# A language-model tower on one core: moving the row-maximum loop by two slots, reordering three engines' work, and weighing the low-rank product with ScalarE and GpSimd

## The reference, cut to what matters

```python
h = einsum('bsk,kh->bsh', concat[pos[s], nest[nesting(x)], seg[segments(x)]], W)     # 32 x 512 x 128
h = h + attn(layernorm(h))       # 8 heads of 16, softmax over 512 keys, no mask
# experts, on the layernorm of h (xf): 4 experts, rank 16
weights = relu(softmax(xf @ gate_w.T) - sigmoid(xf @ thr_w.T) / 4); weights /= sum(weights)
hidden = relu(einsum('ni,ehi->neh', xf, fc1_w))
lo = einsum('neh,ehr->ner', hidden, lora_A)                  # "low" in the kernel
out = einsum('ne,ned->nd', weights, fc2(lora_B(lo)))         # weights are applied to lo in the kernel
h = h + out
```

## Time and profile before

| | before |
|---|---|
| median of 3 runs | 1198.49 us (1197.38 to 1198.84) |
| the profiled execution, own time / span | 1197.47 / 1195.7 us |
| busy: PE, DVE, ACT, POOL | 88%, 80%, 69%, 57% of the span |
| granted TensorE clock, mean of the span | 0.957 (1.00 from 110 to 1150 us) |

### The profile page before, as it was taken

One profiled execution on the slowest core, in us unless ns is written; L12 is line 12 of the kernel. 1 busy time (PEld: TensorE's weight loads), 2 busy tenths in 40 slices (PEclk: granted clock), 3 DMA queues, 4 the chain that ended last, 5 costly groups with the idle time before them and its releaser, 6 DMA issues.

```text
span 1195.7 us, 20256 instructions
## 1 busy us (share of the span) xinstructions
PE 1052.9 (88%) x6158; PEld 393.8 (33%) x6158; DVE 952.5 (80%) x2442; ACT 821.4 (69%) x1578; POOL 681.9 (57%) x684
## 2 busy tenths in 40 slices
PE   5268889999999999999999999999999999999965
PEld 2012233333333333333333333333333333333322
DVE  7399888888888888888888888888888888888322
ACT  2216777777777777777777777777777777776841
POOL 1844575676556665665566665765556656632231
PEclk8558999999999999999999999999999999999986
DMA  2544545554544445555544455545544455541111
GB/s 73 136 100 107 126 105 129 125 121 118 126 120 112 112 119 135 119 121 121 128 114 112 115 122 133 118 120 123 127 109 113 116 130 122 121 98 39 55 56 36
DMA packets 93242, 132.43 MB, mean 111 GB/s; under 512 B 18109, under 2 KB 69822, under 8 KB 86918
## 3 DMA queue, kind: packets, MB, share of 16 engines
q1 hardware_dynamic: 91584, 129.54, 45.1%
q10 hardware_dynamic: 1550, 1.59, 0.5%
HBM read 89.20 MB, written 35.01 MB: 104 GB/s over the span
## 4 chain that ended last, share of the span: by engine, by line
PE 53%; DVE 25%; issue 9%; ACT 8%; DMA 3%; POOL 1%; SPq 0%; POOLq 0%; ACTq 0%; DVEq 0%
PE pv L723 13%; PE mix L733 13%; DVE negmax L1009 10%; PE sc L710 9%; PE mix L787 7%; ACT probs L578 4%; PE mix L770 3%; PE mix L808 3%; PE mix L792 3%; DVE bn L999 2%; DVE qk L994 2%; ACT hid L632 2%; DVE out_sb L1088 2%; DVE h_sb L986 2%; DVE h L1034 2%
## 5 line engine op out<-in xcount | busy, mean ns | idle before, releaser
L1009 DVE TENSOR_REDUCE negmax<-mix 128x1 f32<-128x512 f32 x1024 | 671.9, 680 | 122.7 <-PE mix L733 119.6
L578 ACT ACTIVATE probs<-sc 128x512 f32<-128x512 f32 x1024 | 574.3, 596 | 218.2 <-PE sc L710 214.1
L733 PE MATMUL mix<-kstk,qstk 96*128 96x512 bf16 x1024 | 360.2, 395 | 84.0 <-ACT turned L622 22.4
L710 PE MATMUL sc<-qstk,kstk 120*128 120x512 bf16 x1024 | 361.7, 381 | 1.5 <-ACT probs L578 1.2
L723 PE MATMUL pv<-probs,vals 128*32 128x512 f32 x2048 | 273.8, 601 | 0.0
L733 PEld LDWEIGHTS mix<-kstk,qstk 96*128 96x128 bf16 x1024 | 92.3, 98 | 434.7 <-DVE negmax L1009 179.1
L514 POOL TENSOR_TENSOR ctxh<-ctx_sb,rdenb 128x512 f32<-128x512 f32 x64 | 81.2, 1270 | 221.0 <-DMA rdenb<-rden_dram 220.6
L787 PE MATMUL mix<-xn2T,fc1T_sb 128*128 128x512 f32 x256 | 135.4, 612 | 8.0 <-DVE negmax L1009 8.0
L710 PEld LDWEIGHTS sc<-qstk,kstk 120*128 120x128 bf16 x1024 | 99.7, 98 | 103.7 <-issue 29.8
L494 POOL TENSOR_TENSOR qk<-qk,rstdb 128x512 f32<-128x512 f32 x64 | 81.3, 1272 | 92.0 <-DMA rstdb<-rstd_dram 92.0
L632 ACT ACTIVATE hid<-mix 128x512 f32<-128x512 f32 x128 | 76.1, 596 | 35.4 <-PE mix L787 35.4
(11 more groups left out here) (141 smaller groups left out, 1067.4 us busy)
## 6 DMA issues: line engine op xcount, KB each, us to landing
stack_dram<-pieces SPq DMA_DIRECT2D x192, 128.0 KB
rdenb<-rden_dram SPq DMA_DIRECT2D x64, 256.0 KB
qstk<-stack_dram SPq DMA_DIRECT2D x32, 384.0 KB, 6.6
kstk<-stack_dram SPq DMA_DIRECT2D x32, 384.0 KB, 8.7
rstdb<-rstd_dram SPq DMA_DIRECT2D x32, 256.0 KB, 3.4
qstk<-stack_dram SPq DMA_DIRECT2D x32, 256.0 KB, 7.0
kstk<-stack_dram SPq DMA_DIRECT2D x32, 256.0 KB, 9.2
wrow<-w_dram SPq DMA_DIRECT2D x32, 256.0 KB
```

Of the source, the lines that this page charges most:

```text
L578: act.activation(probs[:, c % 8, i % 2], sc[:, i % RING], ACT.Exp).then_inc(s_exp, 1)
L710: pe.matmul(sc[:, i % RING, :], kstk[0:KROWS, u, h, j * P:(j + 1) * P], qstk[0:KROWS, u, h, :], start=True, stop=True).then_inc(s_score, 1)
L733: pe.matmul(max_bank(m), qstk[0:STK, u, h, j * P:(j + 1) * P], kstk[0:STK, u, h, :], start=True, stop=True).then_inc(s_mxmm, 1)
L1009: dve.tensor_reduce(negmax[:, m // NT, m % NT:m % NT + 1], max_bank(m), AX.X, ALU.max, negate=True).then_inc(s_max, 1)
```

## The change

It has five parts. (1) `MSTART` goes from 8 to 10. (2) PE: `fc1_3` goes to slot 1 and `embed` to slot 2; ACT's relu 3 to slot 1; DVE's `add_pos`, `stats1` and `moments1` of `t+4` go one slot later. (3) ACT: `wT` is copied before `mT`, and `ctx` 0 after the first exponential of slot 12; `mix_user` now names `mT` as the last reader of that bank. (4) `weigh` leaves DVE: ACT copies the product from PSUM to SBUF in slot 4 (`copy_low`), which frees the bank, and POOL multiplies in place after `norm2`. (5) The stacked operands of sequence 0 are loaded in two halves of four heads each, so that its first tiles need the first half only.

```diff
-MSTART = 8
+MSTART = 10
-    ("project", -2), ("embed", 4), ("fc1_3", -3), ("low", -3), ...
+    ("project", -2), ("fc1_3", -3), ("embed", 4), ("low", -3), ...
 ACT_WORK = [
-    (1, 2, "qk", 3, 0), (2, 2, "relu", -3, 3), (3, 1, "qk", 3, 1), (4, 0, "ctx", -1, 1), (5, 2, "xn2T", -2, 0),
+    (1, 1, "relu", -3, 3), (1, 2, "qk", 3, 0), (3, 1, "qk", 3, 1), (4, 0, "low", -3, 0), (4, 0, "ctx", -1, 1), (5, 2, "xn2T", -2, 0),
...
-    (12, 0, "rT", 4, 0), (12, 0, "mT", 1, 0), (12, 0, "ctx", 0, 0), (12, 1, "wT", -2, 0), (13, 1, "relu", -2, 2),
+    (12, 0, "rT", 4, 0), (12, 0, "wT", -2, 0), (12, 0, "mT", 1, 0), (12, 1, "ctx", 0, 0), (13, 1, "relu", -2, 2),
 DVE_WORK = [
-    (2, 1, "add_pos", 4, 0), (3, 0, "stats1", 4, 0), (3, 1, "stats1", 4, 1), (4, 0, "weigh", -3, 0),
-    (5, 0, "moments1", 4, 0), (6, 1, "finish", -3, 0), (7, 1, "invert_den", -1, 0),
+    (3, 0, "add_pos", 4, 0), (4, 1, "stats1", 4, 0), (5, 0, "stats1", 4, 1),
+    (6, 0, "moments1", 4, 0), (6, 1, "finish", -3, 0), (7, 1, "invert_den", -1, 0),
 POOL_WORK = [
-    ("scale", 3, 0), ("add_bias", 3, 0), ("scale", 3, 1), ("rstd2", -2, 0), ("norm2", -2, 0),
+    ("scale", 3, 0), ("add_bias", 3, 0), ("scale", 3, 1), ("rstd2", -2, 0), ("norm2", -2, 0), ("weigh", -3, 0),
...
+            def load_half_heads(g):
+                heads = slice(4 * g, 4 * g + 4)
+                for side in range(2):
+                    sp.wait_ge(s_pcout[side], 48)
+                    for row, p, n in STACK:
+                        dst, src = ((qstk, stack_dram[0, 0, :, p, heads].unsqueeze(1).broadcast_to([HC, n, 4, S])),
+                                    (kstk, stack_dram[0, 1, :, 0:n, heads]))[side]
+                        sp.dma_start(dst[row:row + n * HC, 0, heads, :], src).then_inc(s_half[g][side], 16)
...
+            def weigh(b):                                  # POOL
+                upto(pool, s_lowcp, b)
+                upto(pool, s_win, b, 16)
+                pool.tensor_tensor(low[:], low[:], wrow[:], ALU.mult).then_inc(s_low, 1)
...
+            def copy_low(b):                               # ACT
+                upto(act, s_lomm, b)
+                upto(act, s_outmm, b - 1)
+                act.copy(low[:], aux("low", 1)).then_inc(s_lowcp, 1)
...
-                if m == 0:
+                if m == 0 or b == 0 and m == 16:
                     for side in range(2):
-                        upto(pe, s_stk[side], b, 48)
+                        if b == 0:
+                            pe.wait_ge(s_half[m // 16][side], 48)
+                        else:
+                            upto(pe, s_stk[side], b, 48, 0)
...
-                "low": (low_rank, (s_low, 1, 1)),
+                "low": (low_rank, (s_lowcp, 1, 1)),
-                    if name == "mT" and runs(t - 2):
-                        return t - 2, (s_wT, 1, 1)
                     if name == "mT" and not runs(t + 1):
-                        return t + 4, (s_rT, 1, 1)
+                        return (t - 2, (s_wT, 1, 1)) if t > 0 else (t + 4, (s_rT, 1, 1))
...
-            def weigh(b):                                  # DVE
-                upto(dve, s_lomm, b)
-                upto(dve, s_win, b, 16)
-                upto(dve, s_outmm, b - 1)
-                dve.tensor_tensor(low[:], aux("low", 1), wrow[:], ALU.mult).then_inc(s_low, 1)
```

More of the change, by code:

```diff
@@ L54 @@
 PRODUCTS = [
-    ("project", -2), ("embed", 4), ("fc1_3", -3), ("low", -3), ("none", None), ("xn2T", -2), ("out", -3), ("gates", -2),
+    ("project", -2), ("fc1_3", -3), ("embed", 4), ("low", -3), ("none", None), ("xn2T", -2), ("out", -3), ("gates", -2),
     ("turn_gates", -2), ("fc1_0", -2), ("fc1_1", -2), ("mT", 1), ("q", 4), ("fc1_2", -2), ("k", 4), ("v", 4),
@@ L265, in tower @@
         s_stk = [sem(f"s_stk{a}") for a in "qk"]
+        s_half = [[sem(f"s_half{g}{a}") for a in "qk"] for g in range(2)]
         s_mxmm, s_max = sem("s_mxmm"), sem("s_max")
@@ L287, in tower @@
         s_lomm, s_low = sem("s_lomm"), sem("s_low")
+        s_lowcp = sem("s_lowcp")
         s_outmm, s_out, s_store = sem("s_outmm"), sem("s_out"), sem("s_store")
@@ L333, in store_piece @@
                 if p == 0:
-                    upto(sp, s_stk[side], b - 2, 48)
+                    if b == 2:
+                        sp.wait_ge(s_half[1][side], 48)
+                    upto(sp, s_stk[side], b - 2, 48, 0)
                 sp.dma_start(stack_dram[b % 2, side, :, p].rearrange("c h s -> h c s"),
                              pieces[:, side, p, :]).then_inc(s_pcout[side], 16)
+            def load_half_heads(g):
[6 more added lines that the diff above has]
+                        sp.dma_start(dst[row:row + n * HC, 0, heads, :], src).then_inc(s_half[g][side], 16)
             def load_qstack(b, u):
@@ L412, in _ @@
                 "piece": lambda b, u, part: store_piece(b, *part),
-                "stack": lambda b, u, side: (load_qstack, load_kstack)[side](b, u),
+                "stack": lambda b, u, side: (load_qstack, load_kstack)[side](b, u) if b else load_half_heads(side),
                 "den_in": lambda b, u, _: load_den(b),
@@ L527, in _ @@
                 "v": lambda b, u, _: value(b, u),
+                "weigh": lambda b, u, _: weigh(b),
                 "residual": lambda b, u, side: residual(b, side),
@@ L639, in _ @@
                 "wT": lambda b, u, _: copy_wT(b),
+                "low": lambda b, u, _: copy_low(b),
                 "rT": lambda b, u, _: copy_rT(b),
@@ L877, in step @@
                 for c in range(SLOTS):
-                    if t == -4 and c == 2:
+                    if t == -4 and c == 3:
                         fold_positions()
@@ L1105, in _ @@
                 "gate": lambda b, u, part: (gate_first, gate_second, gate_third, gate_fourth)[part](b),
-                "weigh": lambda b, u, _: weigh(b),
                 "finish": lambda b, u, _: finish(b, u),
@@ L1115, in step @@
                         copy_weights()
-                    if t == -4 and c == 6:
+                    if t == -4 and c == 7:
                         cut_folded()
```

## The result

The changed kernel takes 1143.97 us (median of 4 runs, 1143.02 to 1145.8) where the kernel before took 1197.93 us (4 runs beside it, 1195.48 to 1198.84): a ratio of 0.9554, interval 0.9535 to 0.9573. That is 54.0 us or 4.5% faster. The profiled execution took 1143.9 us, its span 1142.1 us.

A forecast was written before the change was run, and what follows sets the result against it. PE's own stream plus four PE waits bound the kernel. From 1197.47 us, 28 steady steps gave -38.6 and the ends -3.3, making 1155.6; 1.4 added for thin covers gave 1157, range 1148 to 1177.

The forecast's parts named there:

- the four waits: In each steady step PE waits 0.41 us (slot 9), 0.96 (slot 12), 0.67 (slot 15), 0.84 (slot 2): 2.88 in sum.
- lateness at slot 4: Steady step, slot 4: some 0.05 us of lateness goes when DVE loses the `weigh` product.
- rival A: DVE's cut and gate work, moved to slot 10, meets GpSimd products and is stretched; chance 0.17 slight, 0.06 on the cut.
- A1: Slight meeting each step: `hot` with `scale` 0, or gate part 2 with `third` 1; up to 0.5 us, 1171; chance 0.17.
- A2: The cut in slot 10 meets GpSimd; PE waits 2.2 us a step at slot 11: 1218; chance 0.06.
- The ends: Fill and last steps: -2.8 half loads, -2.4 four max tiles, +0.9 step 30, +1.0 last steps: -3.3 us.
- the 28 steps: Steady steps, each shortened by 1.38 us through less waiting at slots 9, 12 and 4: -38.6 us in all.
- the addition: 1.4 us added to the summed time 1155.6 because some work was hidden by only 0.1 to 0.2 us.
- the four max tiles: In the fill, four fewer max tiles ahead of slot 0 of step 0, at 0.60 us each: -2.4 us.
- thin covers: Places in the step where late work stays hidden from PE by only 0.1 to 0.2 us; 1.4 us added.

The follow-up runs named there:

- the last experiment: Changed kernel with `add_pos` and second `add_qk` read earlier, `weigh` back on DVE, `hot` ahead of DVE's last max reduction: 1104.06 us, ratio 0.9234.

## Why the prediction was right, and where it was wrong

**Right: the four waits.** The account of a step by PE's waits held. `fc1_0` lost its lateness; slot 12 lost its wait (0.93 forecast, 0.97 by the experiment that puts the order back); max 1 of slot 3 is late by 1.09 - 0.22 = 0.87 us (0.88 forecast); slot 15 stays at 0.67. 2.88 less 1.54 is 1.34; the step fell by 1.46. The 0.12 between them is PE's own stream: 33.78 - 2.88 = 30.90 before, 32.32 - 1.54 = 30.78 after, which is the step without waits that the last experiment shows (30.77). The prediction gave 0.05 to lateness at slot 4 and left PE's stream as it was, so each step was mis-sized by 0.08: 2.1 us over the 25. (Its terms as written, 0.41, 0.93 and 0.05 less 0.04, add up to 1.35 and not to 1.38; with 1.35 the miss would be 0.11 a step.)

**Right: `weigh` is hidden in the steady steps**, and costs only at the ends. The prediction had 1.0 us for it there; the experiment says some 3.6 in all, most of it (2.4) behind the last `project`. Other parts won some of this back, so that the last line of the table is 0.9.

**Right: rival A's mechanism and its place.** That the cut must not meet GpSimd's products is what decides between the versions: with the cut in slot 8 the same change is 0.6% slower than before. The Trainium skill (SBUF — State Buffer, Who interferes with whom) says which DVE instructions can contend, casts, `tensor_scalar` and those with two SBUF inputs, and that reductions don't. The runs agree: 0.16 to 0.21 us instructions of those kinds stretch to 0.70, 1.00 and 1.08, `hot` from 0.34 to 1.38 and 1.41, and the row maxima keep their mean of 0.68 us. A1 was half right. `hot` did meet `scale` 0, in 15 of 24 steps of the changed kernel, and nothing was given back, since PE waits for nothing behind it. Gate part 2 is what costs, and with GpSimd 1 us later it costs 0.51 us a step ("up to 0.5"); by the rows its meeting begins at 0.3 us of delay (608.51 to 608.80). A2's step, that 1.5 us of further delay decide by the cut, did not occur: with 3 us the cut is not met, and the load of `den` decides.

**Wrong: "The ends", the fill.** This step failed: -5.2 us forecast, -11.5 measured, nearly half of the whole miss (13.1 from 1157 to 1143.9: 6.3 fill, 4.4 the 28 steps, 1.0 the last steps, 1.4 the addition). The mechanisms that it named are there; the term is mis-sized. What the parts are worth in the fill, each from the run that takes it back or does it alone:

| part | forecast | measured |
|---|---|---|
| `MSTART` (alone) | -2.4 | -5.9 |
| half loads (taken back) | -2.8 | -3.0 |
| `embed` later (taken back) | 0 | -2.65 |
| ACT's order (taken back) | 0 | -0.9 |
| `weigh` (taken back) | not split | +0.9 |
| sum | -5.2 | -11.55 (whole change: -11.5) |

The last two values (ACT's order and `weigh`) are no larger than the scatter of such readings: with the same loads, the first max tile starts between 48.81 and 49.74 in the ten profiled versions with half loads. And that the sum meets the whole is in part luck, since the first value depends on the rest: `MSTART` taken back from the changed kernel is worth 7.2 us in the fill (146.92 against 139.72).

I counted the four max tiles that move out of the fill, and carried the edits' steady-step values (0 for `embed`) into a stretch where other things are bare. The cut in the fill makes PE wait 2.90 us in one step of the kernel before and 1.19 with `MSTART = 10`; row 81.35 of the earlier trace rows, which I used as evidence for rival A, was itself the price of the fill and was not put into the sum. The timeline of DVE shows its size: in the kernel before, the cut meets GpSimd in two steps of the fill and takes 2.70 us (from 79.85) and 2.80 (from 107.60), and with `MSTART = 10` alone 1.60 (from 79.68) and 1.45 (from 106.03). These 2.4 us and the 2.4 of the four tiles make 4.8 of the 5.9, by my estimate. Why `embed` in its old slot costs 2.65 us there is shown for 1.0 of it: the longest wait for `add_pos` in the fill is 2.65 us against 1.68 after. The half loads had nearly the right worth by a wrong road: q's first half didn't wait for k's pieces (it is issued at 42.75), and the halves alone bring the first tile forward by 3.7 us (53.15 to 49.49), of which 3.0 reach `project` of step 2.

**Wrong, small: three of the 28 steps.** Steps 2, 28 and 29 won 6.4 us, not 4.1, since their waits differ from those of the equal steps. Which ones they are was not tried. And the 1.4 us added for thin covers: the only cover that failed was that of `hot`, and it cost nothing.

## What to carry to other kernels

Work out a steady step by the lateness of each wait on the bound engine, and check it against the stream that is left when all are gone; but go through the fill by its own waits, since an edit that is worth nothing in the steady state was worth 2.65 us there, and one worth 0.5 us a step 5.9. The parts don't add up: the cut's new slot alone won 20 us, and 60 in the changed kernel, where GpSimd's products run on into the old slot. Before work is moved onto GpSimd, list the small DVE casts, `tensor_scalar` and two-input instructions, and where the moved GpSimd products will stand beside each of them, and ask what PE waits for behind each (the long `hot` cost nothing, the long gate part 2 0.5 us a step); then follow the transfers that queue behind GpSimd's results to whoever waits for them. Two reads of a shared bank, each moved one place ahead of the reduction beside it in DVE's list, were worth some 30 us here (0.9554 to 0.9301 of 1197), more than any part of the change but the cut's new slot.

## What the runs showed of the hardware that I had not expected

- A short wait of PE can cost nearly twice. With 2.12 us of idle PE in a step, the granted clock went from 1.00 to a mean of 0.76 for the next 7 us in most steps (0.38 us matmuls took 0.63), 1.6 us more for the step. In the run with the cut back in slot 8 the same wait was 1.65 us (42.8 us in 26), and the mean granted clock of the span stayed at 0.954 (0.958 after, 0.929 with `weigh` alone); one of its 25 equal steps took 35.84 us instead of 34.21, with a mean granted clock of 0.66 in the 5 us behind the wait.
- Instructions on 128x4 elements are held up as well: the gate's `tensor_scalar`, 0.16 us alone, took 0.70 while a GpSimd product of 128x512 ran. It ended at 648.39, GpSimd's product at 648.37. The meeting costs GpSimd little when DVE is first: `hot` of 0.34 us that started at 266.18 in the changed kernel kept its time, and the product that started at 266.26 took 1.38 instead of 1.27.
- The stacked load was in time after 4.0 us from k's first issue when each transfer had half of the bytes, and after 8.4 when whole.
